# The opening of a fused cross-attention and FP4 feed-forward kernel: rounding masks in PSUM, weights prepared by column group, the order laid out anew

## What is computed

```python
def fp4_quant_dequant(x):
    xb = x.reshape(shape[:-1] + (shape[-1] // BLOCK, BLOCK))
    scale = jnp.maximum(jnp.max(jnp.abs(xb), axis=-1, keepdims=True) / 6.0, 1e-12)
    idx = jnp.searchsorted(_MID, jnp.abs(xb / scale))
    return (_GRID[idx] * jnp.sign(xb / scale) * scale).reshape(shape)

x = x + xattn(layernorm(x), ctx, ctx, Wt, Wp, Wg, Wz, gamma, beta)
n = layernorm(x)
h = silu(fp4(n) @ fp4(w_gate).T) * (fp4(n) @ fp4(w_up).T)      # 1408 columns
x = x + fp4(h) @ fp4(w_down).T
```

## Time and profile before

| | |
|---|---|
| median of 3 runs | 1741.73 us (1741.09 to 1741.89) |
| profiled execution, span | 1739.4 us; no time of its own outside the span is listed for it |
| busy in the span | PE 1682.5 (97%), DVE 1518.6 (87%), ACT 825.6 (47%), POOL 707.2 (41%) |
| chain that ended last | PE 94%, of it L550 52% and L561 25% |
| mean granted TensorE clock | 0.997 of 2.4 GHz |
| HBM read, written | 43.03 MB, 16.78 MB |

### The profile page before, as it was taken

How to read it: one execution, slowest core, us unless ns; L and a number is a source line. 1 busy time by engine, 2 the same in 40 slices (tenths; PEclk the granted TensorE clock), 3 DMA queues, 4 the chain that set the end, 5 groups by cost and what they waited for, 6 DMA issues and landing times.

```text
span 1739.4 us, 27808 instructions
## 1 busy us (share of the span) xinstructions
PE 1682.5 (97%) x8723; PEld 922.4 (53%) x8723; DVE 1518.6 (87%) x2577; ACT 825.6 (47%) x1472; POOL 707.2 (41%) x879
## 2 busy tenths in 40 slices
PE   2789999999999999999999999999999999999999
PEld 1666555555555555555555555555555555555544
DVE  8987888889888888988888898888888988888887
ACT  3656545444445454444554444454544444545322
POOL 6865333334444333444433334443333444433310
PEclk9999999999999999999999999999999999999999
DMA  8123334334344434343434434333434444333321
GB/s 257 34 43 66 88 89 105 88 91 97 78 94 91 94 87 99 89 96 79 93 89 94 98 83 106 75 87 90 104 87 92 96 81 93 91 92 87 76 52 47
DMA packets 412150, 155.86 MB, mean 90 GB/s; under 512 B 383200, under 2 KB 384480, under 8 KB 412128
## 3 DMA queue, kind: packets, MB, share of 16 engines
q1 hardware_dynamic: 396352, 125.17, 33.7%
q10 hardware_dynamic: 15776, 30.41, 5.4%
HBM read 43.03 MB, written 16.78 MB: 34 GB/s over the span
## 4 chain that ended last, share of the span: by engine, by line
PE 94%; DVE 2%; ACT 2%; DMA 1%; issue 1%; POOL 0%; SPq 0%; DVEq 0%; ACTq 0%
PE pairs L550 52%; PE work L561 25%; PE work L500 5%; PE work L512 3%; PE ubank L527 2%; PE work L527 2%; PE pairs L605 1%; PE pairs L500 0%; PE pairs L597 0%; DMA hT_parts<-raw 0%; DMA raw<-in_L_ffn_w_gate 0%; DVE w_rinv L1205 0%; DVE x_in L1223 0%; PE pairs L607 0%; PE pairs L580 0%
## 5 line engine op out<-in xcount | busy, mean ns | idle before, releaser
L550 PE MATMUL pairs<-w_gate_hi,xT_parts 128*128 128x512 f16 (+1 forms) x1536 | 555.4, 362 | 1.8 <-DMA xT_parts<-raw 1.5
L550 PE MATMUL pairs<-w_up_hi,xT_parts 128*128 128x512 f16 (+1 forms) x1536 | 554.7, 361 | 0.0
L561 PE MATMUL work<-w_parts,hT_parts 128*128 128x512 f16 x2079 | 458.9, 379 | 0.9 <-DMA hT_parts<-raw 0.9
L561 PEld LDWEIGHTS work<-w_parts,hT_parts 128*128 128x128 f16 x2079 | 203.5, 99 | 236.1 <-issue 1.1
L550 PE MATMUL pairs<-w_up_lo,xT_parts 128*128 128x512 f16 (+1 forms) x768 | 277.5, 361 | 0.0
L550 PE MATMUL pairs<-w_gate_lo,xT_parts 128*128 128x512 f16 (+1 forms) x768 | 277.4, 361 | 0.0
L550 PEld LDWEIGHTS pairs<-w_gate_hi,xT_parts 128*128 128x128 f16 x1536 | 152.7, 99 | 163.2 <-issue 15.1
L550 PEld LDWEIGHTS pairs<-w_up_hi,xT_parts 128*128 128x128 f16 x1536 | 150.3, 98 | 146.5
L964 ACT ACTIVATE early<-pairs,w_unit 128x512 f32<-128x512 f32 (+1 forms) x192 | 124.9, 651 | 166.3 <-PE pairs L550 166.3
L873 ACT CAST raw<-hq 128x704 f16<-128x704 f32 x126 | 98.1, 779 | 179.5 <-DVE hq L1201 178.7
L1409 DVE SCALAR_TENSOR_TENSOR h<-pairs,w_unit,early 128x512 f32<-128x512 f32 (+1 forms) x192 | 135.0, 703 | 39.9 <-ACT early L964 34.6
(11 more groups left out here) (193 smaller groups left out, 2803.6 us busy)
## 6 DMA issues: line engine op xcount, KB each, us to landing
out<-raw SPq DMA_DIRECT2D x64, 256.0 KB, 2.1
c_in<-in_ctx ACTq DMA_DIRECT2D x29, 512.0 KB, 3.8
x_in<-in_x ACTq DMA_DIRECT2D x29, 512.0 KB, 5.3
...
```

Source lines behind the costliest of these rows:

```text
L550: mm = pe.matmul(pairs[:, pair, n, 0:b - a], xT[s][part][:, k, :], w1[n][wpart][:, k, a:b], start=(k == 0 and part == 0 and wpart == 0), s ...
L561: mm = pe.matmul(obank[:, :], hT[part][:, k, :], w2[wpart][:, k, :], start=(k == 0 and part == 0 and wpart == 0), stop=(k == KH - 1 and pa ...
```

## The change

It alters only the opening, up to the first round of the loop.

1. The mask of a weight rounding is written by ACT as float32r to PSUM (`w_grain`, two areas of `work`, 1024 and 512 columns) instead of bf16 to SBUF. Both halves of the rounding now read mask from PSUM and weights from SBUF and write SBUF.
2. Gate and up are loaded, scaled and rounded by column group (2048, 2048 and 1536 staged columns), in pieces of 512 to 1536; a piece is rounded in bits of 1024, 896 or 512. There are 14 pieces and 24 bits, where there were 12 chunks. Sets go gate and up in turn, group by group, then down.
3. The scaling of the reciprocals by `SNAP_BELOW` goes from POOL (six instructions) to ACT (`weight_snap`, eight).
4. The rounding mask of the first hidden tile has a buffer of its own (`hm`).
5. The calls of the opening stand in another order on all five engines, and waits that stood between them stand in the functions. The first load is a group of gate; x comes third.

```diff
+        w_grain = [work[:, 0:2].rearrange("p a n -> p (a n)"), work[:, 2]]
-        w_sum = work[:].rearrange("p a n -> p (a n)")[:, 0:H]
-        wm = [sb(f"wm{n}", [P, H], BF16)[:, :] for n in range(2)]
...
+        LOADS = [[(a * D // P, b * D // P) for a, b in SPANS] for m in range(2)] + [[(0, HALF), (HALF, WCOLS)]]
+        pieces = []
+        for c in range(GROUPS):
+            for m in range(2):
+                a, b = LOADS[m][c]
+                cuts = (a, b) if c == GROUPS - 1 else (a, a + (2 - m) * D, b)
+                pieces += [(m, c, k, n) for k, n in zip(cuts, cuts[1:])]
+        for k in range(0, WCOLS, H):
+            pieces.append((2, k // HALF, k, k + H))
+        bits = []
+        for n, (m, c, a, b) in enumerate(pieces):
+            rest = 0 if b - a == D or m == 0 and c < 2 and a % (4 * D) == 0 else D
+            cuts = (a, b - rest, b) if rest else (a, b)
+            bits += [(n, k, q) for k, q in zip(cuts, cuts[1:])]
...
         def sets_for_group(c):
-            return KH + SPANS[c][1] // P
+            return 2 * SPANS[c][1] // P
...
+            def load_raw(m, f):
+
+                a, b = LOADS[m][f]
+                if m == 2 and f == 1:
+                    sp.wait_ge(w_rest_done, sets_over(0, HALF))
...
+            def weight_grain(k):
+
+                n, a, b = bits[k]
+                if k == 0:
+                    act.wait_ge(attw_copied, 2)
+                at_least(act, w_r_done, k - 1)
+                act.wait_ge(w_y_done, n + 1)
+                nc.scalar.activation(w_grain[k % 2][:, 0:b - a].bitcast(F32R), staged(pieces[n][0], a, b), ACT.Abs,
+                                     scale=GRAIN).then_inc(w_grain_done, 1)
+
+            def weight_snap(m, f):
+
+                a, b = load_blocks(m, f)
+                act.wait_ge(w_inverse_done[m], f + 1)
+                nc.scalar.activation(w_rinv[m % 2][:, a:b], w_rinv[m % 2][:, a:b], ACT.Identity,
+                                     scale=SNAP_BELOW).then_inc(w_rinv_done[m], 1)
...
-                nc.vector.scalar_tensor_tensor(out=w_sum, in0=wm[n % 2], scalar=GRAIN, in1=staged(m, c * H, H), op0=ALU.max,
-                                               op1=ALU.add).then_inc(w_t_done, 1)
-                dve.wait_ge(w_t_done, n + 1)
-                nc.vector.scalar_tensor_tensor(out=staged(m, c * H, H), in0=wm[n % 2], scalar=GRAIN, in1=w_sum, op0=ALU.max,
-                                               op1=ALU.subtract).then_inc(w_r_done, 1)
+            def weight_round(k):
+
+                n, a, b = bits[k]
+                y, m = staged(pieces[n][0], a, b), w_grain[k % 2][:, 0:b - a]
+                dve.wait_ge(w_grain_done, k + 1)
+                snap_add(y, m, w_t_done)
+                dve.wait_ge(w_t_done, k + 1)
+                snap_back(y, m, w_r_done)
...
+            load_raw(0, 0)
+            load_raw(0, 1)
+            load_ctx(0)
+            load_wz()
             load_x(0)
```

More of the change, by code:

```diff
@@ L72, in build @@
     WCOLS = KD * H
-    WCH = WCOLS // H
     HALF = WCOLS // 2
@@ new lines, in place_of, with load_blocks, pieces_to, first_under @@
+        def place_of(n):
+            return of_matrix[pieces[n][0]].index(n)
+        def load_blocks(m, f):
+            a, b = LOADS[m][f]
+            return a // BLK, b // BLK
+        def pieces_to(m, f):
+            return sum(1 for n in of_matrix[m] if pieces[n][1] <= f)
+        def first_under(n):
+            _, _, a, b = pieces[n]
+            return 1 + max(k for k in of_matrix[0] if pieces[k][2] < b and pieces[k][3] > a)
+        def staged(m, a, b):
+            if m == 0:
+                return raw_flat[:, a:b]
+            if m == 1:
+                return up_staged[:, a:b]
+            return raw_flat[:, 2 * HALF + a:2 * HALF + b] if a < HALF else raw_flat[:, a - HALF:b - HALF]
@@ L348, in sets_before @@
-        def sets_before(n):
-            return sum(1 for m, _, chunk, _ in weight_sets if WCH * m + chunk < n)
+                    weight_sets.append((m, cols, [w1[m][part][:, :, r * P:(r + 1) * P] for part in range(2)]))
+        DOWN_SET0 = len(weight_sets)
+        for r in range(KD):
+            for k0, nk in SETS:
+                cols = [r * H + (k0 + k) * P for k in range(nk)]
+                weight_sets.append((2, cols, [w2[part][:, k0:k0 + nk, r * P:(r + 1) * P] for part in range(2)]))
@@ new lines, in turn_wz, with join_wz @@
+            def turn_wz():
+                pe.wait_ge(diag_made, P // CG)
+                for s in range(HT):
+                    mm = pe.transpose(obank[:, s * P:(s + 1) * P], wz_bd[:, s, :], ident[:, :])
+                mm.then_inc(attw_in_psum, 1)
+            def join_wz():
+                pe.wait_ge(attw_copied, 2)
+                for k in range(HT):
+                    for s in range(HT):
+                        mm = pe.matmul(pairs[:, 1, 0, (k * HT + s) * P:(k * HT + s + 1) * P],
+                                       w_nat[:, 0, s, k * P:(k + 1) * P], wzT[:, s, :], start=True, stop=True)
+                mm.then_inc(attw_in_psum, 1)
```

817 lines of the change are left out of this document (435 added, 382 removed).

## The result

The changed kernel took 1727.45 us (median of 4 runs, 1726.0 to 1728.7) beside 1741.45 of the kernel before: ratio 0.992, 95% interval 0.9906 to 0.9934. That is 14.0 us less, where the prediction had 5.9, and it lies under the stated range. The sign was right, the size was not. The profiled execution spans 1726.1 us, 13.3 less than before.

What follows compares the result with a forecast made beforehand. VectorE's queue up to x_lo was taken to bound the opening. Its terms summed to -2.8 us, first layer matmul 2.3 earlier; with 5.1 of moved PE work, 1741.7 - 7.4 + 1.5 = 1735.8 us, range 1729.5 to 1742.0.

Steps and rivals of the forecast that it cites:

- other waits for POOL: VectorE's queue up to x_lo: waits for POOL other than in the roundings shrink, -1.5 us, between +3 and -5.
- given back: PE from the first layer matmul on: less work to fill gaps, late transposes and clock risk, +1.5 us allowed.
- Masks in PSUM: VectorE's rounding halves L1470: with one SBUF input, eight fall from 16.7 to 13.0 us, -3.7 us.
- Dearer reads from PSUM: VectorE's roundings: PSUM masks cost nothing more to read; upper bound 2.2 us; as a rival 1738.0, chance 0.05.
- Pieces: VectorE ahead of x_lo: one more chunk +3.2 us, nine more instruction pairs +2.5, more scales +0.6.
- normalise2 behind x_lo: VectorE's queue: the second tile's normalise2, 1.30 us, moves behind the first tile's x_lo, -1.3 us.
- VectorE's other idle time: VectorE ahead of x_lo: ACT's cast of the tile comes earlier, -1.5 us, between +3 and -4.
- Moved PE work: PE's opening: more weight sets and u_rows done before the first layer matmul, 5.1 us out of the dense stretch.
- More than counted: Rival, VectorE's opening: both open terms at their lower bounds, -9 instead of -3, 1729.8 us; chance 0.13.
- both open terms: VectorE ahead of x_lo: other waits for POOL and VectorE's other idle time, each taken as -1.5 us.
- Nothing gained: Rival, VectorE's queue: it meets POOL at worse moments and waits for ACT as long, 1740.3 us; chance 0.20.
- Slower: Rival, VectorE's products between the first tile's groups: late down-piece masks from ACT delay them, 1747.8 us; chance 0.12.

Runs made afterwards that it cites:

- a_mask_sbuf: The changed kernel with the rounding mask back in SBUF as bf16 and the first half's sum in PSUM: 1740.6 us, 0.9994 of the kernel before.
- b_bits: The kernel before, old order and SBUF masks, each 1408-column chunk rounded as 896 then 512, mask one bit ahead at most: 1749.0 us.
- b_mask_psum: b_bits with the mask moved to PSUM as float32r and the sum in place in SBUF, still in the old order: 1743.5 us.

## Why the prediction was wrong

The step that failed is the term "other waits for POOL", -1.5: it measured -9.0. It put x_lo at 95.8 where it came at 90.1, and that early, PE's own queue and no longer x_lo sets the first layer matmul. The second miss is "given back", +1.5, which measured -1.1.

- **What bounds it: right in part.** The time went out of PE's idle time in the first 100 us, and VectorE's queue was what kept PE idle. That x_lo and its DMA are the way from it to PE is right for neither kernel as it stands: before, w_max led there too and PE's own queue came level with the DMA; in the changed one PE's queue comes 1.3 us behind. x_lo came 8.5 us earlier, the first layer matmul 7.0 (predicted 2.8 and 2.3).
- **Masks in PSUM, -3.7: right as a term, wrong as a price.** The halves' own wait went from 3.8 to 0.2. (Of the eight L1470 counted, the last starts at 98.53, behind x_lo; it takes 1.62 and adds nothing.) But I took it from the old chunks only and counted nothing for what the waits pass on. In the new order the masks are worth 13.2 us of time: 11.0 us of waits in the halves and 3.2 in the other steps.
- **Dearer reads from PSUM: taken as nothing, right.** Rounding halves of 512 columns take 0.683 and 0.691 with the mask in PSUM (groups below), the same two forms with a bf16 mask in SBUF 0.681 and 0.682. The 65 ns that the Trainium skill's table ("VectorE: DVE Perf Modes", the section on the TRN2 errata) would add do not show.

```profile
L1286 DVE SCALAR_TENSOR_TENSOR raw<-work,raw 128x512 f32<-128x512 f32 x5 | 3.5, 691 | 0.2
L1282 DVE SCALAR_TENSOR_TENSOR raw<-work,raw 128x512 f32<-128x512 f32 x5 | 3.4, 683 | 0.1
...
L1282 DVE SCALAR_TENSOR_TENSOR xn<-xm,xn 128x512 f32<-128x512 bf16 x1 | 0.7, 681 | 0.0
```

- **Pieces, +3.2, +2.5, +0.6: right.** 32 halves at 28.1 us undisturbed against 14 at 22.7 is +5.4, predicted +5.7. Scales and reciprocals moved by under 0.5.
- **First load, -1.1: half.** The first maximum starts at 6.36, not 5.8; VectorE idled 6.88 before, so -0.5.
- **normalise2 behind x_lo, -1.3: within the next term.** 0.54 of it is work, the rest was a wait.
- **Other waits for POOL, -1.5: the step that failed.** They went from 15.3 to 6.3 us, with normalise2's 0.8 out of it some 8 us where I took 1.5. I had bounded it by three lines, 10.2 us, and left out that c_norm's two steps (2.3 us over) and normalise1's (1.8 over) wait as well. And I did not see that the masks' own meetings and POOL's stretched products keep the other steps waiting too: 3.2 us of the other waits come back with the masks in the new order. In the old order they did not (11.8 and 12.2 us). The rest, 5.8 us in the new order with the masks in SBUF, came with the order and the pieces; splitting the chunks in the old order alone took 3.5. Which of the two it is, smaller pieces or other meetings, was not tried apart. No account of these waits is good to better than the 2.4 us by which two profiles of the same kernel differ.
- **VectorE's other idle time, -1.5: wrong.** 14.0 before, 13.6 after, of which the first load is 0.5. The 2.65 ahead of x_lo are gone, as forecast, but VectorE now waits 2.1 for PE (L544), 1.4 for ACT's v_sb and 1.0 for PE (L656). With all terms as measured (-3.6, +5.4, -9.0, -0.5 for normalise2's work, -0.4) the sum is -8.1 of the 8.5 us.
- **From x_lo to the first layer matmul, 3.9 us: 5.0**, because PE came there no earlier.
- **Moved PE work, -5.1: nearly.** PE's busy time ahead of the first layer matmul is 59.1 us, before 54.5, so 4.6. From the first layer matmul to the first output stage were 62.7 us and are 54.5; 2.7 of the 8.2 are less idle.
- **Given back, +1.5: the other way.** PE idle from 100 to 160 us fell from 3.4 to 0.7; only the loop took 1.6 us, and all its idle time is the waits for the hT transposes of the second and third tile (0.69 and 1.10). I had named the transpose of the first tile, and that one is in time. In sum 1.1 us gained.
- **The marks.** Quick halves, output stage early: yes. First layer matmul in 97 to 102 and PE idle near 43: passed, 95 and 35.9. "A loop below 1499" was to show me wrong: it is 1498.21, but at 1.6 us it is no cause.
- **Rivals.** "More than counted" came closest (both open terms at their lower bounds, 1729.8) and still fell 2.3 us short, and not by its own mechanism: one of the two terms went beyond its bound of -5, the other did nothing. It should have had more than 0.13. "Nothing gained" is the time that a_mask_sbuf shows, for the reason given against it. "Slower" is the time of b_bits and b_mask_psum, by a late mask as that rival has it but at another place.
